# Keys of the fourth head between the second and third score tile of each attention block

## Chip, cores and metric

The kernel runs on one core of a Trainium2 chip. The metric is the device time of one execution in microseconds (us), the median of several. The engines are TensorE (PE; its weight loads are shown apart as PEld), VectorE (DVE), ScalarE (ACT), GpSimd (POOL) and SyncE (SP), which here issues the loads of the weights.

## The reference

Four graph layers run one after another over 625 nodes with 512 features and 20,000 edges; each takes a normalised copy of `x` and adds its result to it. The change lies in the third, which has four blocks with attention of four heads of 128 features. One block, cut:

```python
y = cond_layer_norm(x, cond, ...)                    # scale and bias made from a condition
q = (y @ wq + bq).reshape(N, H, Dh) * Dh ** (-0.5)
k = (y @ wk + bk).reshape(N, H, Dh)
v = (y @ wv + bv).reshape(N, H, Dh)
scores = einsum('ehd,ehd->eh', q[src], k[dst])       # one score per edge and head
attn = softmax of the scores over the edges of one src
out = segment_sum(attn[:, :, None] * v[dst], src)
x = x + out.reshape(N, D) @ wo + bo
y = cond_layer_norm(x, cond, ...)
x = x + relu(y @ m_w1 + m_b1) @ m_w2 + m_b2
```

## The kernel before

The edge sums are done densely: an earlier stage builds a 625 x 625 matrix of edge counts, and attention is that of all nodes to all nodes with a mask made of the logarithm of the counts. Nodes come in five tiles of up to 128 (`NT = 5`), features in four (`KT = 4`); a head is one feature tile. Every fp32 product is made of three passes: each operand is kept as a rounded high part and a low part (the rest), and high x high, high x low and low x high are summed. So every operand that is made on the chip costs a copy on ACT (high) and a subtraction on DVE or POOL (low).

The third layer is `pe_l2`, `act_l2`, `dve_l2` and `pool_l2`: one program for each engine, a loop over four blocks (`it`), written out in full, each with its own fixed order. Semaphores that only count up tie them: `big_full` (PE has filled a PSUM buffer), `big_read` (DVE has read it), `split_done` (the low part of a weight tile is there), `shi_up` (its high part is), `qkhi_up`, `exp_up`, `rden_up`, `pn_up` and others. Three large PSUM buffers are used in turn, in the order of one list, `BLOCK_BIG`; use number u waits until use u-3 has been read (`free_big`).

In a block, PE makes the values, then eight projections q0 to q3 and k0 to k3 (one head each, 24 matmuls), then goes through the list `ATT`, which `attention_order(True)` builds. It has, for 20 tiles (head, node tile), a score tile S (6 matmuls), three steps behind it the transposes T of the same tile's probabilities (5 matmuls), and for each head two products with the values, PVa and PVb. It starts S0, S1, S2, S3, T0, S4, T1, S5, ... ACT follows `ATT_ACT`, where T comes ahead of S in a step: S0, S1, S2, T0, S3, T1, ...

What one tile passes through: PE scores; DVE adds the mask, writes the tile to `pbuf` and keeps its minimum (L2073); ACT takes exp with the sum of the rows (L1473); DVE inverts the sum (L2078), placed behind the next tile's L2073; POOL scales the tile (L1268, it counts `pn_up`); PE transposes it (L1649, waits for `pn_up`); ACT copies the high part (L1478) and DVE takes the low part (L2082).

A projection passes through ACT (L1465, high part with the bias) and DVE (L2062, low part). The weights come by DMA into four staging buffers, ACT copies the high part into a ring of six slots (`high`, L1514), POOL makes the low part (`rest`, L1327). In ACT's program each of the eight projections is followed by one such copy: WK2, WK3, WO0 to WO3, W1_0 and, behind k3, W1_1 (tile 1 of `m_w1`). In POOL's program these low parts, W1_1 the last of them, stand ahead of the loop over the 20 scalings:

```python
                rests(WO + NT - 2, 0, KT + 4 - NT)
                for k in range(HEADS * NT):
                    wait_apart(g, rden_up, it * HEADS * NT + k + 1)
```

(WO3, W1_0 and W1_1 are made in the first line.) SP loads a weight tile as soon as the low part of the tile four places ahead of it has been made (`stage`).

Of the kernel before, what the change touches and what calls it, by code (L numbers as in the profile page):

```python
# [13 lines left out]
ALU = mybir.AluOpType  # L14
# [27 lines left out]
HEADS = 4  # L42
# [31 lines left out]
def attention_order(scores_first):  # L74
# [4 lines left out]
    for k in range(HEADS * NT + LAG):  # L79
# [3 lines left out]
        for what, behind in (("PVa", PVA_AT), ("PVb", PVB_AT)):  # L83
            if kk >= behind and (kk - behind) % NT == 0:
# [2 lines left out]
    return steps + [("PVb", HEADS - 1)]  # L87


ATT = attention_order(True)  # L90
ATT_ACT = attention_order(False)


BLOCK_BIG = (FIRST_NORM + [f"q{h}" for h in range(HEADS)] + [f"k{h}" for h in range(HEADS)]
             + [f"{a}{b}" for a, b in ATT] + norm_order(1) + [f"m{o}" for o in range(KT)])
L3_BIG = [f"l3_{t}" for t in range(NT)] + ["asr"]

# [57 lines left out]
def wide(ap640):  # L155

    return ap640[:, 0:NW].rearrange("p (h n) -> p h n", h=2)
# [6 lines left out]
def build(nc, a, out):  # L164
    ctx = ExitStack()
    with ctx:
# [147 lines left out]
        def bwide(u):  # L314
            return big[buf(u)][:, :, 0:HW]
# [1113 lines left out]
        def act_l2(act, high):  # L1429
            def turned(ln, t, b):  # L1430
                act_turned(act, ln, t, b)

            for it in range(BLOCKS):
                nb, nr = it * len(BLOCK_BIG), it * len(BLOCK_ROW)

                def highs(q, first, last):
                    for i in range(first, last):
                        high(S_BLK + q + i, ringpart(RING_BLK + q + i)[0], it)

                def value(t):  # L1440
                    act.wait_ge(row_read, ROWBLK[f"v{t}"] + nr + 1)
                    act.activation(vrow[:, 0, t, :], vbuf[:, t % 2, :], ACT.Copy).then_inc(vhi_up, 1)

                if it:
                    act.wait_ge(row_full, ROWB + nr)
                    highs(WV, 2, KT)
                    turned(0, 1, it)
                    act.wait_ge(row_read, ROWB + nr)
                    act_bias(act, it)
                    highs(WQ, 0, 1)  # L1450
                    turned(0, 2, it)
                    highs(WQ, 1, 2)
                for t in range(NT):
                    value(t)
                    if t + 3 < NT + (not it):
                        turned(0, t + 3 - (not it), it)
                    if not it and t < 2:
                        highs(WQ, t, t + 1)
                highs(WQ, 2, KT)
                highs(WK, 0, 2)  # L1460
                for i, to in enumerate((qT, kT)):
                    for h in range(HEADS):
                        u = BIGBLK["qk"[i] + str(h)]
                        act.wait_ge(big_full, u + nb + 1)
                        act.activation(wide(to[:, 0, h, :]), bwide(u), ACT.Identity,  # L1465
                                       bias=bqk[:, i, bass.ds(it * KT + h, 1)]).then_inc(qkhi_up, 1)
                        n = i * HEADS + h + 2
                        highs((WK, WO, W1)[n // KT], n % KT, n % KT + 1)

                for what, k in ATT_ACT:  # L1470
                    if what == "S":
                        act.wait_ge(big_read, BIGBLK[f"S{k}"] + nb + 1)
                        act.activation(pbuf[:, k % 4, 0:NW], pbuf[:, k % 4, 0:NW], ACT.Exp, bias=nsmax[:, k:k + 1],  # L1473
                                       scale=-1.0, accum_out=den[:, k:k + 1]).then_inc(exp_up, 1)
                    elif what == "T":
                        u = BIGBLK[f"T{k}"]
                        act.wait_ge(big_full, u + nb + 1)
                        act.activation(pT[:, 0, :, (k % NT) * P:(k % NT + 1) * P], bflat(u).rearrange("p (k n) -> p k n", k=NT),  # L1478
                                       ACT.Copy).then_inc(phi_up, 1)
                    else:  # L1480
                        u, at = BIGBLK[f"{what}{k}"], PV_COLS[what]
                        act.wait_ge(big_full, u + nb + 1)
                        act.activation(qT[:, 0, k, at], big[buf(u)][:, 0, 0:at.stop - at.start], ACT.Copy).then_inc(ohi_up, 1)
                for t in range(NT):
                    turned(1, t, it)
                    if t == 2:
                        act.wait_ge(row_full, ROWBLK["wo4"] + nr + 1)
                    if t >= 2:
                        highs((W1, W1, W2)[t - 2], (2, 3, 0)[t - 2], (3, 4, 1)[t - 2])
                highs(W2, 1, 2)  # L1490
                if it == BLOCKS - 1:
                    act.wait_ge(big_read, BIGBLK[f"S{HEADS * NT - 1}"] + nb + 1)
                    for t in range(NT):
                        act.activation(mask[:, t, :], mask[:, t, :], ACT.Identity, bias=flag[:, 3, t:t + 1], scale=DH ** -0.5).then_inc(m3_up, 1)


                for o in range(KT):
                    act.wait_ge(big_read, BIGBLK[f"m{o}"] + nb + 1)
                    act.activation(kT[:, 0, o, 0:NW], rbuf[:, o % 2, 0:NW], ACT.Copy).then_inc(hhi_up, 1)
                    if o < 2:  # L1500
                        highs(W2, 2 + o, 3 + o)
                    for i in ((), (), (0,), (1, 2, 3))[o] if it < BLOCKS - 1 else ():
                        high(S_BLK + PERBLK + i, condw[:, i, :], it)
                if it < BLOCKS - 1:
                    for i in range(2):
                        high(S_BLK + S_PERBLK + i, ringpart(RING_BLK + i)[0], it)
                    turned(0, 0, it + 1)
# [174 lines left out]
        def pe_l2(pe, turn_norm):  # L1682
# [6 lines left out]
            for it in range(BLOCKS):  # L1689
# [20 lines left out]
                turn_y(0, 4, it)  # L1710
                for t in (3, 4):
                    values(t)
                for i in range(2):
                    for h in range(HEADS):
                        u = BIGBLK["qk"[i] + str(h)]
                        free_big(pe, u, nb)
                        q = (WQ, WK)[i] + h
                        pe.wait_ge(split_done, S_BLK + q + 1 + ns)
                        wide_mm(pe, u, sum([parts(wcol(RING_BLK + q, k), both(yT, k)) for k in range(KT)], [])).then_inc(big_full, 1)
                def row_terms(name, t, left, w, pieces):  # L1720

                    pe.wait_ge(split_done, S_BLK + w + pieces[-1] + 1 + ns)
# [21 lines left out]
                for what, k in ATT:  # L1744

                    if (what, k) == ("PVa", HEADS - 1):
                        row_begin("wo", 0, qT, WO)
                    elif (what, k) == ("PVb", HEADS - 1):
                        out_end(0)
                        row_begin("wo", 1, qT, WO)  # L1750
                    u = BIGBLK[f"{what}{k}"]
                    free_big(pe, u, nb)
                    if what == "S":
                        h, t = k // NT, k % NT
                        pe.wait_ge(big_read, BIGBLK[f"k{h}"] + nb + 1)
                        wide_mm(pe, u, parts(nodes_of(qT, h, t), both(kT, h))).then_inc(big_full, 1)
                    elif what == "T":
                        pe.wait_ge(pn_up, it * HEADS * NT + k + 1)
                        turn(pe, u, pbuf[:, k % 4, :], NT).then_inc(big_full, 1)
                    else:  # L1760
                        at = PV_COLS[what]
                        last = k * NT + at.stop // P - 1
                        pe.wait_ge(big_read, BIGBLK[f"T{last}"] + nb + 1)
                        pe.wait_ge(vlo_up, (it + 1) * NT)
                        row_mm(pe, big[buf(u)][:, 0, 0:at.stop - at.start],
                               sum([parts([vrow[0:KEYS[st], s, st, k * DH:(k + 1) * DH] for s in range(2)],
                                          [pT[0:KEYS[st], s, st, at] for s in range(2)]) for st in range(NT)], [])).then_inc(big_full, 1)
# [234 lines left out]
        def dve_l2(dve, tile_sums, tile_moments, tile_stats, entry_stats, f32, relu_rest, l3_norm):  # L2002
            dve.wait_ge(mask_up, NT)
            norm_tile, centred, scaled, turned_rest = dve_first(dve, f32)
            for it in range(BLOCKS):
# [49 lines left out]
                    turned_rest(0, t, it)  # L2055
                    values(t - 1)
                values(4)
                for i, to in enumerate((qT, kT)):
                    for h in range(HEADS):
                        u = BIGBLK["qk"[i] + str(h)]  # L2060
                        dve.wait_ge(qkhi_up, it * 2 * HEADS + i * HEADS + h + 1)
                        dve.scalar_tensor_tensor(wide(to[:, 1, h, :]), bwide(u), bqk[:, i, bass.ds(it * KT + h, 1)],  # L2062
                                                 wide(f32(to[:, 0, h, :])), ALU.add, ALU.subtract).then_inc(big_read, 1)
                heads = it * HEADS * NT
                for what, k in ATT + [("last", 0)]:
                    if what == "S":
                        u = BIGBLK[f"S{k}"]
                        t = k % NT
# [456 lines left out]
```

## Time and profile before

| | us |
|---|---|
| runs | 952.76, 954.74, 957.96 |
| median | 954.74 |
| the profiled execution | 953.18 |
| its span | 951.3 |
| PE busy | 850.3 (89%) |
| DVE busy | 660.6 (69%) |
| POOL busy | 515.8 (54%) |
| ACT busy | 457.3 (48%) |

The mean granted clock of TensorE was 0.964 of full speed. The four blocks lie between about 190 and 825 us of the span. The view of waits tells who released an engine that stood idle; the timeline gives each engine's instructions in order of time, with the idle time ahead of them; the view of windows gives busy time and clock of a stretch.

### The profile page before, as it was taken

The page shows a single profiled execution, that of the slowest core. Times are in us where ns is not written, and L with a number is a line of the kernel's source. Part 1 is how long each engine was busy: PE and PEld are TensorE (multiplying, and loading weights), DVE is VectorE, ACT ScalarE, POOL GpSimd, SP SyncE. Part 2 cuts the span into 40 slices and gives each one's busy share as a digit, 9 for nine tenths or more (in the row PEclk, how much of TensorE's full clock was granted, in tenths as well). Part 3 has the DMA queues.
Part 4 walks back from the last instruction along what each step waited for, and adds up shares of the span by engine and source line. Part 5 has one row for each costly group of instructions (what it writes and reads, how often), then busy time and mean ns, then how long its engine had stood idle before and what let it go on. Part 6 is the DMA issues. An engine that isn't in the chain of part 4 may idle for free.

```text
span 951.3 us, 18275 instructions
## 1 busy us (share of the span) xinstructions
PE 850.3 (89%) x6760; PEld 744.5 (78%) x6760; DVE 660.6 (69%) x1305; ACT 457.3 (48%) x764; POOL 515.8 (54%) x601
## 2 busy tenths in 40 slices
PE   3899869989999899999988999989999998888886
PEld 2788757878998787989786989878798978765456
DVE  8999888782466685266676346577427667679896
ACT  5777563233565233466233456423437615245664
POOL 7677624257632466843176753256674319447771
PEclk9999978999999999999999999999999999978899
DMA  5000001142200024300016220002330002100111
GB/s 131 32 0 0 23 23 23 47 100 78 79 1 1 23 70 111 111 23 2 1 36 169 75 67 1 2 23 80 100 114 21 1 1 78 34 1 29 43 57 55
DMA packets 49362, 44.34 MB, mean 47 GB/s; under 512 B 6014, under 2 KB 37154, under 8 KB 49300
## 3 DMA queue, kind: packets, MB, share of 16 engines
q1 hardware_dynamic: 47492, 40.21, 14.7%
q10 hardware_dynamic: 1808, 3.31, 1.8%
q8 instruction: 38, 0.62, 0.3%
q14 instruction: 24, 0.20, 0.1%
HBM read 42.04 MB, written 1.33 MB: 46 GB/s over the span
## 4 chain that ended last, share of the span: by engine, by line
PE 61%; DVE 21%; issue 6%; ACT 5%; POOL 3%; DVEq 2%; DMA 2%; ACTq 0%; SPq 0%; POOLq 0%
PE psum L1631 24%; PE psum L1625 16%; PE psum L1725 11%; PE psum L1649 5%; DVE arena L2082 2%; ACT arena L1478 2%; DMA bias<-in_L_gnn_m_b 2%; PE psum L849 1%; DVE arena L927 1%; DVE stats L2210 1%; PE psum L1673 1%; DVE hot_dst L964 1%; DVEq L2314 1%; DVE hot_dst L2309 1%; DVE xn L2223 1%
## 5 line engine op out<-in xcount | busy, mean ns | idle before, releaser
L1268 POOL TENSOR_SCALAR acc<-acc,rden,flag 128x628 f32<-128x628 f32 x80 | 69.8, 873 | 111.0 <-DVE rden L2078 110.5
L1725 PE MATMUL psum<-ringw,arena 128*128 128x512 f32 (+1 forms) x480 | 119.0, 397 | 3.7 <-DVE arena L2090 2.5
L1631 PE MATMUL psum<-arena 128*128 128x384 f32 (+5 forms) x675 | 115.7, 324 | 0.0
L1631 PE MATMUL psum<-ringw,arena 128*128 128x512 f32 (+1 forms) x418 | 99.7, 391 | 17.0 <-POOL ringw L1327 5.2
L1625 PEld LDWEIGHTS psum<-arena,ringw 128*128 128x128 f32 x768 | 113.0, 190 | 0.4
L1625 PE MATMUL psum<-arena,ringw 128*128 128x314 f32 x768 | 113.3, 309 | 0.0
L1631 PEld LDWEIGHTS psum<-arena 128*128 128x128 f32 (+1 forms) x675 | 105.0, 189 | 6.7 <-DVE arena L2082 1.1
L1725 PEld LDWEIGHTS psum<-ringw,arena 128*128 128x128 f32 (+1 forms) x480 | 86.9, 186 | 24.8 <-DVE arena L2090 3.5
L1631 PEld LDWEIGHTS psum<-ringw,arena 128*128 128x128 f32 x418 | 75.3, 203 | 34.1 <-issue 15.4
L1649 PE MATMUL psum<-ident,acc 128*128 128x128 f32 (+1 forms) x560 | 81.0, 275 | 19.1 <-DVE acc L1991 15.3
L1625 PE MATMUL psum<-arena 128*128 128x314 f32 (+1 forms) x480 | 88.2, 322 | 6.3 <-DVE arena L2082 5.6
L2062 DVE SCALAR_TENSOR_TENSOR arena<-psum,cols,arena 128x628 fp32r<-128x628 f32 x32 | 27.9, 872 | 88.0 <-ACT arena L1465 88.0
L1649 PEld LDWEIGHTS psum<-ident,acc 128*128 128x128 f32 (+1 forms) x560 | 65.9, 140 | 28.6 <-DVE acc L1991 18.7
L1327 POOL TENSOR_TENSOR ringw<-raw,ringw 128x512 fp32r<-128x512 f32 x56 | 72.2, 1297 | 28.7 <-ACT ringw L1514 28.7
L1320 POOL TENSOR_SCALAR veps<-mv 128x1 f32<-128x1 f32 x60 | 14.4, 240 | 131.9 <-DVE mv L2214 130.4
L1625 PEld LDWEIGHTS psum<-arena 128*128 128x128 f32 (+1 forms) x480 | 70.3, 187 | 15.0 <-DVE arena L2082 13.0
L2082 DVE TENSOR_TENSOR arena<-psum,arena 128x640 fp32r<-128x640 f32 x80 | 65.0, 817 | 15.8 <-ACT arena L1478 15.8
L1378 POOL TENSOR_TENSOR hot_dst<-hot_dst,w_part 128x160 bf16<-128x160 bf16 x120 | 58.2, 512 | 27.0 <-DVE hot_dst L2309 27.0
L1327 POOL TENSOR_TENSOR ringw<-xn,ringw 128x512 fp32r<-128x512 f32 x49 | 64.9, 1338 | 11.1 <-ACT ringw L1514 10.9
L1473 ACT ACTIVATE acc<-acc,nsmax 128x628 f32<-128x628 f32 x80 | 65.2, 815 | 9.2 <-DVE nsmax L2073 8.2
L2073 DVE CUSTOM_DVE_ANT_0 acc<-psum,mask 128x628 f32<-128x628 f32 x80 | 63.8, 801 | 0.0
L1631 PE MATMUL psum<-arena,ringw 128*128 128x314 f32 x384 | 62.1, 327 | 0.0
(283 smaller groups left out, 1834.2 us busy)
## 6 DMA issues: line engine op xcount, KB each, us to landing
raw<-in_L_gnn_m_w SPq DMA_DIRECT2D x16, 256.0 KB
xn<-in_L_gnn_m_w SPq DMA_DIRECT2D x16, 256.0 KB
raw<-in_L_gnn_wv SPq DMA_DIRECT2D x8, 256.0 KB
xn<-in_L_gnn_wv SPq DMA_DIRECT2D x8, 256.0 KB
raw<-in_L_gnn_wq SPq DMA_DIRECT2D x8, 256.0 KB
xn<-in_L_gnn_wq SPq DMA_DIRECT2D x8, 256.0 KB
raw<-in_L_gnn_wk SPq DMA_DIRECT2D x8, 256.0 KB
xn<-in_L_gnn_wk SPq DMA_DIRECT2D x8, 256.0 KB
```

What stands on the lines that cost most here:

```text
L1268: g.tensor_scalar(pbuf[:, k % 4, 0:NW], pbuf[:, k % 4, 0:NW], rden[:, k:k + 1], flag[:, 1, k % NT:k % NT + 1], ALU.mult, ALU.mult).then_in ...
L1327: g.tensor_tensor(to[1], staged[slot(n)], to[0].bitcast(F32), ALU.subtract).then_inc(split_done, 1)
L1378: ins = g.tensor_tensor(hot_dst[:, b, :, (i + 1) * WIN:(i + 2) * WIN], hot, w_part[:, i, :, bass.ds(gr, 1)].broadcast_to([P, CH, WIN]), AL ...
L1473: act.activation(pbuf[:, k % 4, 0:NW], pbuf[:, k % 4, 0:NW], ACT.Exp, bias=nsmax[:, k:k + 1], scale=-1.0, accum_out=den[:, k:k + 1]).then_ ...
L1478: act.activation(pT[:, 0, :, (k % NT) * P:(k % NT + 1) * P], bflat(u).rearrange("p (k n) -> p k n", k=NT), ACT.Copy).then_inc(phi_up, 1)
L1625: ins = pe.matmul(big[buf(u)][0:l.shape[1], h, 0:HW], l, r[:, h * HW:(h + 1) * HW], start=(i == 0), stop=(i == len(terms) - 1))
L1631: ins = pe.matmul(to, l, r, start=(i == 0), stop=(i == len(terms) - 1))
L1649: ins = pe.transpose(bflat(u)[0:KEYS[k], k * P:(k + 1) * P], src[:, k * P:k * P + KEYS[k]], ident[:, :])
L1725: ins = pe.matmul(brow(ROWBLK[f"{name}{t}"])[0:KEYS[t], :], l, r, start=(pieces[0] + i == 0), stop=(pieces[-1] == KT - 1 and i == len(term ...
L2062: dve.scalar_tensor_tensor(wide(to[:, 1, h, :]), bwide(u), bqk[:, i, bass.ds(it * KT + h, 1)], wide(f32(to[:, 0, h, :])), ALU.add, ALU.sub ...
L2073: dve.tensor_tensor_reduce(wide(pbuf[:, k % 4, :]), bwide(u), wide(mask[:, t, :]), -DH ** -0.5, 3e38, ALU.add, ALU.min, nsmax[:, k:k + 1]) ...
L2082: dve.tensor_tensor(pT[:, 1, :, t * P:(t + 1) * P], bflat(u).rearrange("p (k n) -> p k n", k=NT), f32(pT[:, 0, :, t * P:(t + 1) * P]), ALU ...
```

## The change

k3, the keys of the last head, leaves the row of projections and becomes a step of the attention lists, between S1 and S2. In `BLOCK_BIG` it moves the same way. The body of a projection becomes a function on PE, ACT and DVE, called in the loop over `QK` (now seven) and in the loop over `ATT` or `ATT_ACT`. On ACT that body includes the weight copy that follows a projection. `pool_l2` and SP's program are not touched.

```diff
+
 ATT = attention_order(True)
+ATT.insert(2, ("k", HEADS - 1))
 ATT_ACT = attention_order(False)
-
-
-BLOCK_BIG = (FIRST_NORM + [f"q{h}" for h in range(HEADS)] + [f"k{h}" for h in range(HEADS)]
+ATT_ACT.insert(2, ("k", HEADS - 1))
+QK = [("q", h) for h in range(HEADS)] + [("k", h) for h in range(HEADS - 1)]
+
+
+BLOCK_BIG = (FIRST_NORM + [f"q{h}" for h in range(HEADS)] + [f"k{h}" for h in range(HEADS - 1)]
              + [f"{a}{b}" for a, b in ATT] + norm_order(1) + [f"m{o}" for o in range(KT)])
...
-                for i, to in enumerate((qT, kT)):
-                    for h in range(HEADS):
-                        u = BIGBLK["qk"[i] + str(h)]
-                        act.wait_ge(big_full, u + nb + 1)
-                        act.activation(wide(to[:, 0, h, :]), bwide(u), ACT.Identity,
-                                       bias=bqk[:, i, bass.ds(it * KT + h, 1)]).then_inc(qkhi_up, 1)
-                        n = i * HEADS + h + 2
-                        highs((WK, WO, W1)[n // KT], n % KT, n % KT + 1)
+                def projected(what, h):
+                    i, to = {"q": (0, qT), "k": (1, kT)}[what]
+                    u = BIGBLK[f"{what}{h}"]
+                    act.wait_ge(big_full, u + nb + 1)
+                    act.activation(wide(to[:, 0, h, :]), bwide(u), ACT.Identity,
+                                   bias=bqk[:, i, bass.ds(it * KT + h, 1)]).then_inc(qkhi_up, 1)
+                    n = i * HEADS + h + 2
+                    highs((WK, WO, W1)[n // KT], n % KT, n % KT + 1)
+
+                for what, h in QK:
+                    projected(what, h)
 
                 for what, k in ATT_ACT:
-                    if what == "S":
+                    if what == "k":
+                        projected(what, k)
+                    elif what == "S":
...
-                for i in range(2):
-                    for h in range(HEADS):
-                        u = BIGBLK["qk"[i] + str(h)]
-                        free_big(pe, u, nb)
-                        q = (WQ, WK)[i] + h
-                        pe.wait_ge(split_done, S_BLK + q + 1 + ns)
-                        wide_mm(pe, u, sum([parts(wcol(RING_BLK + q, k), both(yT, k)) for k in range(KT)], [])).then_inc(big_full, 1)
+                def projected(what, h):
+                    u = BIGBLK[f"{what}{h}"]
+                    free_big(pe, u, nb)
+                    q = {"q": WQ, "k": WK}[what] + h
+                    pe.wait_ge(split_done, S_BLK + q + 1 + ns)
+                    wide_mm(pe, u, sum([parts(wcol(RING_BLK + q, k), both(yT, k)) for k in range(KT)], [])).then_inc(big_full, 1)
+
+                for what, h in QK:
+                    projected(what, h)
...
+                    if what == "k":
+                        projected(what, k)
+                        continue
                     u = BIGBLK[f"{what}{k}"]
                     free_big(pe, u, nb)
...
+                for what, h in QK:
+                    projected(what, h)
                 heads = it * HEADS * NT
                 for what, k in ATT + [("last", 0)]:
+                    if what == "k":
+                        projected(what, k)
                     if what == "S":
```

(The last piece is DVE's; its `projected` holds the wait for `qkhi_up` and the instruction of L2062, unchanged.)

## Rows read from the trace of the kernel before

**Rows 1.** The page: its head and its part 1 (busy time, share, instructions).

```profile
span 951.3 us, 18275 instructions
...
PE 850.3 (89%) x6760; PEld 744.5 (78%) x6760; DVE 660.6 (69%) x1305; ACT 457.3 (48%) x764; POOL 515.8 (54%) x601
```

**Rows 2.** The page, part 4: the chain that ended last, by engine.

```profile
PE 61%; DVE 21%; issue 6%; ACT 5%; POOL 3%; DVEq 2%; DMA 2%; ACTq 0%; SPq 0%; POOLq 0%
```

**Rows 3.** Timeline of PE, block 1: start, us, engine, line, operation, [idle before, releaser].

```profile
377.39 28.32 PE L1625 MATMUL psum<-arena,ringw 128*128 128x314 f32 x192
405.55 3.93 PE L1625 MATMUL psum<-arena 128*128 128x314 f32 x24
410.44 0.74 PE L1649 MATMUL psum<-ident,acc 128*128 128x128 f32 x5 [0.95 <-POOL acc L1268]
```

**Rows 4.** Waits of PE, whole span: total us, times, longest us.

```profile
PE psum L1649 <- POOL acc L1268: 3.9, 4, 1.1
```

**Rows 5.** Timeline of PE, start of attention in blocks 0 and 3.

```profile
252.47 3.97 PE L1625 MATMUL psum<-arena 128*128 128x314 f32 x24
257.52 0.74 PE L1649 MATMUL psum<-ident,acc 128*128 128x128 f32 x5 [1.08 <-POOL acc L1268]
...
717.68 0.74 PE L1649 MATMUL psum<-ident,acc 128*128 128x128 f32 x5 [0.93 <-POOL acc L1268]
```

**Rows 6.** Timeline of ACT: one row of block 0, three of block 1.

```profile
253.99 1.28 ACT L1473 ACT_TABLE_LOAD   x1
...
405.75 0.79 ACT L1465 ACTIVATE arena<-psum,cols 128x628 fp32r<-128x628 f32 x1 [2.22 <-PE psum L1625]
406.43 0.62 ACT L1514 ACTIVATE ringw<-raw 128x512 fp32r<-128x512 f32 x1
408.20 0.82 ACT L1473 ACTIVATE acc<-acc,nsmax 128x628 f32<-128x628 f32 x1 [1.15 <-DVE nsmax L2073]
```

**Rows 7.** Timeline of DVE, block 1.

```profile
406.57 0.87 DVE L2062 SCALAR_TENSOR_TENSOR arena<-psum,cols,arena 128x628 fp32r<-128x628 f32 x1 [2.65 <-ACT arena L1465]
407.36 0.80 DVE L2073 CUSTOM_DVE_ANT_0 acc<-psum,mask 128x628 f32<-128x628 f32 x1
...
409.15 0.16 DVE L2078 RECIPROCAL rden<-den 128x1 f32<-128x1 f32 x1 [0.25 <-ACT acc L1473]
```

**Rows 8.** Timeline of POOL, block 1 (the last row holds three scalings).

```profile
407.13 1.29 POOL L1327 TENSOR_TENSOR ringw<-raw,ringw 128x512 fp32r<-128x512 f32 x1 [2.23 <-ACT ringw L1514]
409.42 2.73 POOL L1268 TENSOR_SCALAR acc<-acc,rden,flag 128x628 f32<-128x628 f32 x3 [1.00 <-DVE rden L2078]
```

**Rows 9.** Timeline of SP's queue, block 1: first and last issue and the next.

```profile
404.93 3.86 SPq L1159 DMA_DIRECT2D raw<-in_L_gnn_m_w  x2
479.68 1.57 SPq L1159 DMA_DIRECT2D xn<-in_L_gnn_m_w  x2
```

**Rows 10.** Chain of work, block 1, behind the first transposes: start, us, what.

```profile
411.21 0.72 ACT arena L1478
411.95 0.84 DVE arena L2082
412.83 1.14 PE psum L1625 x6
```

**Rows 11.** Windows: length, busy us by engine, PEclk, DMA share, GB/s.

```profile
405.55:410.44 4.89, 3.91 (x27) 3.43 (x25) 3.62 (x10) 3.40 (x7) 2.31 (x3) 1.00 0.29 101
429.79:442.42 12.63, 12.16 (x87) 11.53 (x86) 8.92 (x23) 8.47 (x18) 4.38 (x6) 1.00 0.01 2
480.00:484.00 4.00, 4.00 (x20) 4.00 (x19) 0.89 (x2) 1.64 (x3) 4.00 (x4) 0.57 0.46 131
512.00:516.00 4.00, 2.24 (x9) 1.44 (x9) 3.96 (x7) 1.57 (x3) 3.82 (x5) 1.00 0.74 173
875.00:878.00 3.00, 1.70 (x8) 0.86 (x6) 2.96 (x7) 1.98 (x3) 3.00 (x3) 1.00 0.05 2
878.00:883.00 5.00, 4.67 (x15) 2.58 (x15) 4.53 (x13) 2.47 (x4) 3.17 (x3) 0.66 0.00 1
```

**Rows 12.** Timeline of PE, block 1: the product with `m_w1`.

```profile
480.13 15.69 PE L1631 MATMUL psum<-arena,ringw 128*128 128x314 f32 x96
```

More of the change, by code:

```diff
@@ L2057, in dve_l2, with projected @@
                 values(4)
[L2058 to L2063, printed above, removed]
+                def projected(what, h):
+                    i, to = {"q": (0, qT), "k": (1, kT)}[what]
+                    u = BIGBLK[f"{what}{h}"]
+                    dve.wait_ge(qkhi_up, it * 2 * HEADS + i * HEADS + h + 1)
+                    dve.scalar_tensor_tensor(wide(to[:, 1, h, :]), bwide(u), bqk[:, i, bass.ds(it * KT + h, 1)],
+                                             wide(f32(to[:, 0, h, :])), ALU.add, ALU.subtract).then_inc(big_read, 1)
+                for what, h in QK:
+                    projected(what, h)
                 heads = it * HEADS * NT
                 for what, k in ATT + [("last", 0)]:
+                    if what == "k":
+                        projected(what, k)
                     if what == "S":
```

## The prediction

> **What bounds the kernel now.** I read the page's head and its chain first. TensorE (PE) is busy for 89% of a 951.3 us span, and 61% of the chain that ended last lies on it [rows 1, 2]. So the first question for any edit is what it does to PE's idle time. Next I read PE's timeline around the start of attention in block 1 [rows 3]. The eight projections of q and k run from 377.39 to 405.55 without a gap, 28.16 us, so 3.52 us each. The first score tiles S0 to S3 take 3.93 us, 0.98 each. Then PE stands still for 0.95 us until the first transpose T0 starts at 410.44, released by GpSimd (POOL), which has to scale the first probability tile. The view of waits says the same of all four blocks: four such stalls, 3.9 us in all, 1.1 the longest [rows 4]; blocks 0 and 3 show 1.08 and 0.93 [rows 5]. This one stall per block is all that the change can win here: once T0 runs, PE is busy for 12.16 of 12.63 us in a later stretch of the same loop [rows 11].
>
> **Why T0 is late.** I take the other engines' rows of block 1 and count each from the start of S0 (405.55), which is also the end of the last projection. ScalarE (ACT) turns out k3's high part at +0.20, then makes the high part of the weight tile W1_1 at +0.88 and takes exp of S0 at +2.65 [rows 6]. VectorE (DVE) makes k3's low part at +1.02, reduces S0 at +1.81 and inverts its sum at +3.60 [rows 7]. POOL makes the low part of W1_1 at +1.58 (1.29 us long) and scales tile 0 at +3.87 [rows 8]; T0 follows the start of that scaling by 1.02, at +4.89. The projection k3 and its two copies thus stand ahead of S0 on DVE and ACT, and PE has only S1 to S3 to cover the chain from S0 to T0.
>
> **The change, part by part.** I count from the end of k2 (E2), where S0 now starts. Before, T0 starts at E2 + 3.52 + 4.89 = 8.41; in block 0, where S0 starts at 252.47 and T0 at 257.52 [rows 5], at 3.52 + 5.05 = 8.57.
> - *PE order.* S0 and S1 end at 1.97, k3 at 1.97 + 3.52 = 5.49, S2 and S3 at 7.45. k3 needs k2's PSUM buffer read: DVE's copy ends 1.02 + 0.87 = 1.89 after k2, so in time. Nothing is added; the same instructions run in another order, at zero cost in PE's work. As cover for the chain from S0 it is ideal.
> - *DVE and ACT.* S0's chain is as before (exp +2.65, inverse +3.60), now counted from E2, while PE works on k3. k3's high part falls at 5.49 + 0.20 = 5.69, its low part at 6.51 to 7.38, S2's reduction directly behind it, done near 8.2, S3's near 9.0. On ACT, exp of S1 is done by about 4.5, so it delays nothing, and in block 0 the table load of 1.28 us [rows 6] lies there too, hidden by k3. There is only one such load at the exponentials, so mixing Identity and exp costs nothing further.
> - *The copy of W1_1 moves with k3.* In ACT's program each projection is followed by one weight copy; k3's is W1_1. It now comes after exp of S1 and after k3's own copy. POOL's program is unchanged: it has the low part of W1_1 ahead of the scaling of tile 0. So POOL waits for ACT's copy with tile 0's scaling queued behind that wait, and PE's T0 waits for the scaling. This is the wait that takes the place of the one removed. POOL can start W1_1 at 5.49 + 1.58 = 7.07, ends it at 8.36 and starts scaling then; T0 starts 1.02 later, at 9.38.
> - *Sum.* 9.38 against 8.41 is +0.97 us in blocks 1 to 3, against 8.57 it is +0.81 in block 0: 3 x 0.97 + 0.81 = +3.7 us. PE's idle time ahead of T0 becomes 9.38 - 7.45 = 1.93 us where it was 0.95. The bounds of POOL's turn-round are -0.05 (back-to-back instructions overlap a little) to +0.1 (the gap of 0.10 us between the inverse and the scaling in [rows 7, 8], if it comes on top), so the sum lies between +3.5 and +4.1.
> - *After T0.* The next late step hangs on T0 itself: ACT copies it at +0.77, DVE takes the rest at +1.51 and S5 starts at +2.39 [rows 10]; so the loop runs the same distance behind T0 as before. Nothing is won back there: S2 and S3 are reduced before T0 in both orders.
> - *SP's queue.* The load of the tile W2_1 waits for W1_1's buffer and goes out about 2 us later against the end of the projections. It is in the pair issued from 404.93 on [rows 9], and no other load of the weights is issued in the trace until 479.68, some 70 us later, so that is covered. Were it not, it would cost those 2 us at W2 at most.
> - *Clock.* The longer stall could drop PE's granted clock. At the present stall of 0.95 it stays at 1.00 [rows 11], and so it does over 512 to 516, where PE is idle for 1.76 of 4.00 us. It falls, to 0.57 over 480 to 484, behind a passage in which PE waits for DVE; and to 0.66 over 878 to 883, where the 3 us before held 1.30 idle and work on a part of the array. So the cost is between nothing and a fall to the lower level (1.2 of 2.4 GHz) in each block. That is worth 15.69 - 96 x 28.32/192 = 1.53 us [rows 3, 12]. I take nothing, since the row of 512 to 516 is nearest in idle time, and keep 4 x 1.53 = 6.1 for the range.
>
> The page "TensorE: Matmul & The Clock Gate" of the Trainium skill, section "Architectural detail: the array is 16x 32x32, not 1x 128x128", says that the queues of ACT and GpSimd are strictly first in, first out; by it tile 0's scaling can't slip past W1_1, by a rule of freer order the saving of the second rival would stand. [...]
>
> **Rivals.**
> - *The clock falls in the stall ahead of T0* (slower by over 0.5%). Its place is the 1.93 us idle before T0 in each block; its price 1.53 us where it happens, and it decides once it happens in one or more blocks: +3.7 + 1.53 = +5.2 with one, +9.8 with all four, near 964. For it: the fall near 878 behind only 1.30 us idle [rows 11]. Against it: 512 to 516, and that full-array work stands directly on both sides of the stall.
> - *The cover works and POOL doesn't hold it back* (faster). T0 would start as soon as PE has done S3, at 7.45: -0.96 in three blocks, -1.12 in block 0, -4.0 us, near 950. For it: S0's chain is done by then, as its scaling could start at 3.87. Against it: POOL's place for W1_1, which would have to be reached before ACT's copy. I see no way to that.
> - *The change moves nothing measurable* (-1 to +1 us): POOL's delay is taken up again in the loop, as POOL is busy for only 4.38 of 12.63 us there. Against it: the loop is tied to T0 by ACT and DVE, not to POOL.
>
> **How the numbers follow.** The profiled execution took 953.18 us, 1.9 more than its span; with +3.7 it is 956.9. The median of the runs shown is 954.74, with +3.7 it is 958.4. I take the middle, 957.6. Chances: forecast 0.72, clock 0.15, nothing 0.08, cover works 0.05. About 0.5% (4.8 us) is what a measurement of this kernel can tell from no change, and my sum lies below that. Slower by over that: the clock rival's 0.15, and 0.05 for the upper end of the sum. Faster by over it: 0.02, as even the full saving of 4.0 stays under the bound. Within: 0.78. The range reaches from 952.5 (no effect, with the spread of the runs from 952.76 to 957.96) to 964.0 (the clock falling in all four blocks, 957.6 + 6.1).
>
> **What would show it.** In the changed kernel: POOL's low part of W1_1 starts some 1.6 us after k3's end and tile 0's scaling directly behind it, without a wait; PE's idle time before T0 is near 1.9 us and is still put down to POOL's scaling; S0's exp lies under k3 on PE; the tile loop from T0 on has the same spacing; the clock over it is 1.00. Wrong would be a T0 directly behind S3, a clock under 1.00 after T0, or a stall of PE ahead of k3.

## The result: 965.6 us against 953.8, outside the range

The changed kernel took 965.64 us (median of 4 runs, 962.75 to 967.94), the kernel before 953.75 beside it: ratio 1.0112, interval 1.0088 to 1.0136. A later measurement gave 1.0119 (1.0102 to 1.0136). So it is slower by some 11 us where 3.7 were forecast, and lies above the range's upper end of 964.0. The profiled execution took 967.94 us, its span 966.1.

The page of the changed kernel, its head, part 1, and the row of granted clock of part 2 (40 slices of the span, in tenths):

```profile
span 966.1 us, 18275 instructions
...
PE 859.2 (89%) x6760; PEld 753.4 (78%) x6760; DVE 659.9 (68%) x1305; ACT 457.0 (47%) x764; POOL 513.9 (53%) x601
...
PEclk9999989999999899999999999989999998988899
```

The instructions are the same 18275. DVE, ACT and POOL are busy for as long as before, to 2 us [rows 1]; PE is busy for 9 us longer with the same 6760 matmuls. That is the first sign of a lower clock; the other 6 us of the longer span are idle time. PE's timeline at the start of attention in block 1, the rows that answer to [rows 3]:

```profile
406.95 1.92 PE L1634 MATMUL psum<-arena 128*128 128x314 f32 x12
408.90 3.78 PE L1634 MATMUL psum<-arena,ringw 128*128 128x314 f32 x24
412.52 1.92 PE L1634 MATMUL psum<-arena 128*128 128x314 f32 x12
416.37 1.14 PE L1658 MATMUL psum<-ident,acc 128*128 128x128 f32 x5 [1.94 <-POOL acc L1272]
417.16 1.92 PE L1634 MATMUL psum<-arena 128*116 128x314 f32 x6
```

S0 and S1, k3, S2 and S3, then 1.94 us idle, then T0. T0 and S4, behind it, last 1.14 and 1.92 us; the same two steps took 0.74 and 1.11 to 1.12 us in the kernel before and in block 0 of this one. The view of waits of PE, the answer to [rows 4]:

```profile
PE psum L1658 <- POOL acc L1272: 7.8, 4, 2.0
```

And POOL's timeline, the answer to [rows 8]:

```profile
414.10 1.27 POOL L1331 TENSOR_TENSOR ringw<-raw,ringw 128x512 fp32r<-128x512 f32 x1 [4.28 <-ACT ringw L1523]
415.36 2.57 POOL L1272 TENSOR_SCALAR acc<-acc,rden,flag 128x628 f32<-128x628 f32 x3
```

POOL stands for 4.28 us in front of W1_1, and the scalings follow it without a wait. DVE had inverted tile 0's sum long before (the answer to the last of [rows 7]):

```profile
410.55 0.16 DVE L2098 RECIPROCAL rden<-den 128x1 f32<-128x1 f32 x1 [0.25 <-ACT acc L1482]
```

That is 3.60 us after the start of S0, as forecast, and 4.8 us before the scaling starts.

**Where the time is.** I laid the traces side by side at fixed points of each block: the first projection (P), T0, the start of the last group of ident transposes of attention (TL), the product with `m_w1` (M), the product with `m_w2` behind it, and the next block's P. Three traces of each kernel stand behind the table (the two profiled ones and those of later runs); each entry is the sum of a stretch over the four blocks (three for the last but one), mean of three traces, in us.

| stretch | before | after | more |
|---|---|---|---|
| start to P of block 0 | 224.7 | 224.9 | 0.2 |
| P to T0 | 132.3 | 136.1 | 3.8 |
| T0 to TL | 184.9 | 188.3 | 3.4 |
| TL to M | 94.5 | 94.7 | 0.3 |
| M | 61.8 | 64.2 | 2.5 |
| behind M to the next P | 107.4 | 108.7 | 1.3 |
| behind the last M to the end | 148.2 | 148.2 | 0.0 |

The sum is 11.5. The two profiled executions alone differ by 14.8, of which 1.75 arise before the first block, where the kernels are the same.

P to T0 is the wait that was forecast. The rest lies in stretches in which TensorE's granted clock is lower for longer: from T0 to TL it is at the lower level for 10.2 us in each trace of the changed kernel, and never in the kernel before. Windows of the changed kernel (length, busy us by engine, PEclk, DMA share, GB/s): T0 of block 0, T0 of block 1, and the start of M in block 0, where the kernel before has 0.57 over the four us of its fall:

```profile
259.00:263.00 4.00, 2.64 (x19) 2.42 (x20) 2.21 (x5) 2.94 (x6) 2.68 (x4) 1.00 0.23 66
416.00:420.00 4.00, 3.63 (x17) 3.62 (x18) 1.76 (x5) 1.58 (x4) 1.93 (x3) 0.57 0.27 70
326.00:334.00 8.00, 5.19 (x23) 5.01 (x24) 4.46 (x8) 2.75 (x5) 6.63 (x7) 0.61 0.20 66
```

Each fall in the blocks goes to the lower level (1.2 of 2.4 GHz) and lasts 3.4 us, or 6.8. The changed kernel falls behind T0 in blocks 1, 2 and 3 in all three traces, never in block 0; the kernel before never does.

### The profile page after: what moved, and what is told of

It is laid out like the page before. It is cut to its first block, busy times and chain, and to the rows that moved or that the text cites. A ratio compares the mean times of both kernels' runs of the same rounds, so it can differ in the third digit from the quotient of the medians.

```text
span 966.1 us, 18275 instructions
## 1 busy us (share of the span) xinstructions
PE 859.2 (89%) x6760; PEld 753.4 (78%) x6760; DVE 659.9 (68%) x1305; ACT 457.0 (47%) x764; POOL 513.9 (53%) x601
## 4 chain that ended last, share of the span: by engine, by line
PE 59%; DVE 19%; POOL 6%; issue 6%; ACT 4%; DVEq 3%; DMA 1%; SPq 1%; ACTq 0%; POOLq 0%
PE psum L1640 23%; PE psum L1634 17%; PE psum L1737 9%; PE psum L1658 5%; POOL ringw L1331 3%; DVE arena L2102 2%; ACT arena L1487 2%; DVE arena L931 1%; PE psum L853 1%; PE psum L1682 1%; DVE stats L2230 1%; DVEq L2334 1%; DVE hot_dst L2329 1%; DVE hot_dst L968 1%; DVE z L2327 1%
## 5 line engine op out<-in xcount | busy, mean ns | idle before, releaser
L1737 PE MATMUL psum<-ringw,arena 128*128 128x512 f32 (+1 forms) x480 | 119.1, 397 | 4.2 <-DVE arena L2110 2.5
L1640 PE MATMUL psum<-ringw,arena 128*128 128x512 f32 (+1 forms) x418 | 105.2, 407 | 17.0 <-POOL ringw L1331 6.5
L1634 PE MATMUL psum<-arena,ringw 128*128 128x314 f32 x768 | 114.2, 310 | 0.1
L1640 PEld LDWEIGHTS psum<-arena 128*128 128x128 f32 (+1 forms) x675 | 104.9, 189 | 7.7 <-DVE arena L2102 1.1
L1640 PEld LDWEIGHTS psum<-ringw,arena 128*128 128x128 f32 x418 | 79.9, 214 | 34.7 <-issue 15.3
L1658 PE MATMUL psum<-ident,acc 128*128 128x128 f32 (+1 forms) x560 | 83.9, 282 | 22.5 <-DVE acc L2006 14.7
L1634 PE MATMUL psum<-arena 128*128 128x314 f32 (+1 forms) x480 | 90.6, 328 | 5.5 <-DVE arena L2102 5.3
L1658 PEld LDWEIGHTS psum<-ident,acc 128*128 128x128 f32 (+1 forms) x560 | 68.6, 145 | 31.6 <-DVE acc L2006 17.1
L1634 PEld LDWEIGHTS psum<-arena 128*128 128x128 f32 (+1 forms) x480 | 73.3, 194 | 12.6 <-DVE arena L2102 11.6
L1426 ACT ACTIVATE arena<-psum 128x512 fp32r<-128x512 f32 x40 | 23.8, 594 | 85.4 <-PE psum L1658 85.3
L1640 PE MATMUL psum<-arena,ringw 128*128 128x314 f32 x384 | 64.1, 334 | 0.0
```

What stands on the lines that cost most here:

```text
L1426: act.activation(yT[:, 0, :, t * P:(t + 1) * P], bflat(u)[:, 0:D].rearrange("p (k n) -> p k n", k=KT), ACT.Copy).then_inc(yhi_up, 1)
L1634: ins = pe.matmul(big[buf(u)][0:l.shape[1], h, 0:HW], l, r[:, h * HW:(h + 1) * HW], start=(i == 0), stop=(i == len(terms) - 1))
L1640: ins = pe.matmul(to, l, r, start=(i == 0), stop=(i == len(terms) - 1))
L1658: ins = pe.transpose(bflat(u)[0:KEYS[k], k * P:(k + 1) * P], src[:, k * P:k * P + KEYS[k]], ident[:, :])
L1737: ins = pe.matmul(brow(ROWBLK[f"{name}{t}"])[0:KEYS[t], :], l, r, start=(pieces[0] + i == 0), stop=(pieces[-1] == KT - 1 and i == len(term ...
```

## The experiments

My theory after the result: (1) POOL's order sets T0, (2) the clock falls because PE then stands idle, and (3) neither needs k3 to be where it is. The rivals: DVE or ACT hold T0, as k3 is in their queues too; the fall comes from the kind of work; the later falls are chance.

### Both kernels again

> The kernel before, once more, for its clock. Theory A (the further falls of the clock belong to the change): the trace shows the lower level for about 68 us in all as the first one, none behind T0 and none at the start of a block's values. Theory B (they depend on how the falls happen to lie in an execution): other places, and a total that differs by 10 us or more between two executions of one kernel.

It took 955.63 us. No fall behind T0; a fall at the end of block 0 that the first trace doesn't have; 56 us at the lower level in all, against 68 in the first.

> The changed kernel once more. Both theories: 1.94 us idle ahead of T0 in each block, as that is set by the order of POOL. Theory A: the clock falls behind T0 in three or four blocks again and the lower level lasts about 88 us in all. Theory B: it falls there in one or two blocks or none, and the total lies elsewhere between 68 and 95 us.

965.87 us, idle time ahead of T0 as before, falls behind T0 in blocks 1 to 3, 92 us at the lower level. So neither theory in its pure form: the falls behind T0 belong to the change and come back in the same blocks; the total over the span differs by 12 us between the two executions of the kernel before.

> The kernel before, a third trace, to part chance from the change in the later stages. If the longer falls of the clock at the product with m_w1 belong to the change, the four stretches of that product take 61 to 62 us in all here, as in the two earlier traces (61.9, 60.7), against 63.6 to 64.6 of the changed kernel. If they are chance, this trace may show 63 or more.

957.81 us. The four M take 62.6 us, between the two groups, with one long fall of 6.8 us in block 1. So long falls at M are possible without the change.

> The changed kernel in five rounds beside the kernel before, for the size of the loss. From the two traces of each: longer waits ahead of T0 3.7 us, falls of the clock behind T0 3.3 us, longer falls at the product with m_w1 about 2.7, later parts of the blocks about 1.4: 11 us, ratio 1.0115. If the last two are chance of single executions, the ratio is near 1.0075.

Ratio 1.0119 (1.0102 to 1.0136), 968.06 against 956.42: the larger figure holds. Its four M take 64.6 us (64.5 and 63.6 in the two earlier traces), T0 to TL 188.3 as in those.

### POOL's order

```diff
-                rests(WO + NT - 2, 0, KT + 4 - NT)
+                rests(WO + NT - 2, 0, KT + 3 - NT)
                 for k in range(HEADS * NT):
+                    if k == 1:
+                        rests(W1, 1, 2)
```

> The changed kernel with POOL's low part of W1_1 put behind the scaling of tile 0 instead of ahead of it. Theory 1 (POOL's queue holds T0 back): T0 follows S3 at once, the stall ahead of T0 is under 0.2 us and no fall of the clock starts there. T1 then waits: the inverse of tile 1 stands behind S2's reduction on DVE, about 8.3 us after the end of k2, so T1 starts near 9.4 and some 0.4 us per block remain of the 0.96 against before. Time 2 us under before (near 952), some 14 under the changed kernel. Rival (T0 is held by DVE or ACT, whose queues also got k3 ahead of S2): the stall stays at 1.5 us or more and the time stays near 965.

Ratio 0.9977 (0.9963 to 0.9992) with 955.81 against 957.22: faster than the kernel before. Its PE in block 1, from S2 and S3 on, and its POOL:

```profile
409.92 1.92 PE L1636 MATMUL psum<-arena 128*128 128x314 f32 x12
411.87 0.77 PE L1660 MATMUL psum<-ident,acc 128*128 128x128 f32 x5
```

```profile
408.23 0.86 POOL L1274 TENSOR_SCALAR acc<-acc,rden,flag 128x628 f32<-128x628 f32 x1 [1.00 <-DVE rden L2100]
411.51 1.27 POOL L1333 TENSOR_TENSOR ringw<-raw,ringw 128x512 fp32r<-128x512 f32 x1 [2.41 <-ACT ringw L1525]
412.77 1.87 POOL L1274 TENSOR_SCALAR acc<-acc,rden,flag 128x628 f32<-128x628 f32 x2
```

POOL scales tile 0 while PE works on k3, and T0 follows S3 at once. P to T0 is 32.14 us against 33.04, T0 to TL 46.9 against 46.2, as tile 1's scaling now waits for W1_1. No clock falls behind T0. DVE and ACT, whose order was left, didn't hold T0: that rival is out. Over the four blocks P to TL is 1.0 us shorter than in the kernel before; the ratio says 2.2, and the rest of the lead isn't placed.

> The kernel before with POOL's low part of W1_1 behind the scaling of tile 0, k3 in its old place. If the lead of the kernel with POOL's order changed came from that order itself, this is faster by some 2 us too. Mine: it does nothing, as POOL stands idle for 1.0 us there between W1_1 and the scaling: stall ahead of T0 0.95 us, ratio 1.000 within 0.002.

Ratio 1.0009 (0.9988 to 1.0030). The order of POOL alone gains nothing; it needs k3 in its new place. T0 to TL is longer by 0.26 us a block here. The four M take 63.4 us in this trace, although nothing that idles PE was added.

### The wait moves with k3

k3 is put one place later, behind S2 (`insert(3, ...)` in both lists), POOL as in the changed kernel.

> k3 behind S2 as in the better kernel, but POOL's order as it was, W1_1 ahead of tile 0's scaling. Theory (the wait follows k3 through the copy of W1_1): POOL starts W1_1 1.58 us after the end of k3 (6.47 us after k2), ends it at 9.34 and T0 starts at 10.36, with 2.9 us idle ahead of it: 1.95 us later than in the kernel before in each block, 7.7 us in all, falls of the clock behind T0 in three or four blocks (3.3 to 4.4 us) and more later, 968 to 974. Rival (some other chain holds T0): T0 no later than in the changed kernel.

966.19 against 956.54 us, ratio 1.0110 (1.0066 to 1.0153). T0 of block 1:

```profile
416.41 1.30 PE L1658 MATMUL psum<-ident,acc 128*128 128x128 f32 x5 [2.81 <-POOL acc L1272]
```

The cause is confirmed: k3 one place later makes the stall longer by 0.9 us, one score tile. P to T0 grows by 1.8 us over the kernel before where I had 1.95. The clock falls at T0 in all four blocks, in blocks 1 to 3 within the stall itself, and twice for 6.8 us: T0 to TL costs 6.5 us more than before, where 3.3 to 4.4 were forecast. The time is still lower than forecast (it rests on two runs), as the later stages had few falls: M takes 62.1 us in all, and the stretch behind the last M 145.5 against 148.2.

### Idle time without k3

The kernel before, with two instructions of no use on POOL:

```diff
                 rests(WO + NT - 2, 0, KT + 4 - NT)
+                for i, c in enumerate([512, 256]):
+                    g.tensor_tensor(rbuf[:, i, 0:c], z[:, 0, 0:c], z[:, 1, 0:c], ALU.subtract)
```

> The kernel before, its order unchanged, with two instructions of no use (512 and 256 columns, 1.3 and about 0.65 us) on POOL behind the low part of W1_1 and ahead of the scaling of tile 0. They end about 1 us after the scaling could have started, so PE stands still for about 1.9 us ahead of T0, as in the changed kernel. Theory 1 (it is the idle time alone that counts, not where k3 is made): 3.8 us for the waits, and the clock falls behind T0 in some blocks, some 3 us more: 960 to 965 against 954 to 957. Rival (the fall needs k3 between the score tiles): no fall behind T0, only the 3.8 us.

> The same with 512 and 128 columns: about 0.6 us later, so 1.5 us idle ahead of T0. Theory 1 with a fall that needs nearly 2 us of idle time: +2.4 us and no fall behind T0. If the clock falls here too, the bound lies between 0.95 and 1.5 us.

> The kernel before with two idle instructions of 512 columns on POOL ahead of the scaling of tile 0: about 2.5 us idle ahead of T0, +6 us for the waits. If a longer stall means a surer fall, the clock falls behind T0 in block 0 too (four falls, 4.4 us). If block 0 is spared again, it is not the length of the stall that spares it.

T0 of block 1 in the kernels late by half, by one and by two:

```profile
414.21 0.74 PE L1651 MATMUL psum<-ident,acc 128*128 128x128 f32 x5 [1.58 <-POOL acc L1270]
```

```profile
415.23 1.18 PE L1651 MATMUL psum<-ident,acc 128*128 128x128 f32 x5 [1.88 <-POOL acc L1270]
```

```profile
416.79 1.29 PE L1651 MATMUL psum<-ident,acc 128*128 128x128 f32 x5 [2.40 <-POOL acc L1270]
```

| kernel | idle ahead of T0, block 1 | falls behind T0 | ratio to before |
|---|---|---|---|
| before | 0.95 | none | 1 |
| late by half | 1.58 | none | 1.0058 (1.0038 to 1.0077) |
| late by one | 1.88 | blocks 1 to 3 | 1.0083 (1.0063 to 1.0104) |
| changed kernel | 1.94 | blocks 1 to 3 | 1.0119 (1.0102 to 1.0136) |
| late by two | 2.40 | all four | 1.0119 (1.0070 to 1.0168) |
| k3 behind S2, POOL old | 2.81 | all four | 1.0110 (1.0066 to 1.0153) |

So idle time alone makes the clock fall, with k3 in its old place, in the same blocks as in the changed kernel. Ahead of T0 the step lies between 1.6 and 1.9 us in blocks 1 to 3, and block 0 follows with a longer stall; each kernel that was added has one trace, and the last two ratios rest on two runs each. The length isn't all that decides: block 0 holds its clock behind 1.86 us (late by one) and 1.94 to 1.97 (changed kernel), and at other places of the program shorter pieces are followed by a fall (below). In its trace the kernel late by one copies the changed kernel stretch by stretch (P to T0 33.98 us, T0 to TL 47.3 in blocks 1 to 3). That execution is the slowest of its four, though, and the median is 965.50 us where the changed kernel has 968.06 beside the same kernel before. So it is shown that the falls come from the idle time, and not that the whole loss does. Late by half was forecast at +2.4 us; it has no fall behind T0 and still lost 5.5. Its trace has two falls of 6.8 us at M, 63.6 us in all.

### The stall filled

```diff
                     elif what == "T":
+                        if k == 0:
+                            row_mm(pe, big[buf(u)][:, 0, 0:HW], [(yT[:, 0, 0, 0:P], yT[:, 0, 0, 0:HW])] * 12)
                         pe.wait_ge(pn_up, it * HEADS * NT + k + 1)
```

> The changed kernel with 12 matmuls of 314 columns of no use (about 1.8 us at full clock) put ahead of T0, into the buffer that T0 then overwrites. PE is busy where it stood idle, nothing else moves. If the clock's fall behind T0 comes from the idle time: no fall there, and the stretch from T0 to the last transposes is as long as in the kernel before (46.3 us) in all blocks; the time falls by 3.3 us and by what of the later falls hangs on it, to 957 to 962. If the fall hangs on something else (the kind of work ahead of it), it stays and the time is 965 or a little more.

Ratio 1.0061 (1.0043 to 1.0079), 962.76 against 957.22 us, where the changed kernel has 1.0119; the forecast was 957 to 962. Block 1:

```profile
413.21 2.01 PE L1640 MATMUL psum<-arena 128*128 128x314 f32 x12
415.06 0.76 PE L1658 MATMUL psum<-ident,acc 128*128 128x128 f32 x5
```

T0 comes as late as in the changed kernel (P to T0 33.97 us), but from T0 to TL all four blocks take 46.2: work of no use that keeps PE from idling wins back half the loss. It still loses 5.8 us where the waits are 3.6. The other 2.2 aren't placed: its trace is of one of the two fastest of ten executions (958.65 us). In it the stretches from TL to the next P are longer than before, by 2.4 us in all, and the stretch behind the last M is shorter by 2.9.

### The better version

k3 behind S2, and POOL's low part of W1_1 behind the scaling of tile 1 (`if k == 2`).

> The changed kernel with k3 one place later, behind S2 instead of S1, on all engines, and POOL's low part of W1_1 behind the scaling of tile 1. T0 directly behind S3 (7.45 us after the end of k2, before 8.41), the inverse of tile 1 no longer behind k3 on DVE, so T1 near 9.3. S4 waits for k3's buffer to be read, till 8.4. S5 near 10.3 instead of 10.8: 0.5 us per block, 2 us in all under the kernel before, ratio 0.998. Rival (the loop takes every lead back, as DVE and ACT bound the first tiles): ratio 1.000.

Ratio 0.9968 (0.9955 to 0.9982), 954.10 against 956.42 us: faster than both kernels. PE in block 1:

```profile
410.34 1.04 PE L1636 MATMUL psum<-arena 128*128 128x314 f32 x6
411.22 0.71 PE L1660 MATMUL psum<-ident,acc 128*128 128x128 f32 x5
412.29 1.13 PE L1636 MATMUL psum<-arena 128*116 128x314 f32 x6 [0.36 <-DVE arena L2079]
```

T0 follows S3; S4 waits 0.36 us for k3's buffer, as worked out. P to T0 is 31.97 us against 33.04 and T0 to TL 46.4 against 46.2, which is 0.87 us a block and 3.5 in all; the ratio says 3.1. The lead is kept by the loop, so the rival (DVE and ACT take it back) is out.

## Why the prediction was wrong

- *PE's order, DVE and ACT*: right. S0's chain took 3.60 us to the inverse, k3 started without a wait, and DVE and ACT delayed nothing.
- *The copy of W1_1 moves with k3 and holds tile 0's scaling*: right, in mechanism and size. POOL started W1_1 7.15 us after E2 (406.95) where 7.07 was worked out, T0 came 9.42 after it (9.38), idle 1.94 (1.93). Measured 3.8 us, forecast 3.7.
- *After T0*: right on the order of work (PE's steps have the same distances in block 0), wrong on time, by the next point.
- *Clock*: this is the step that failed. I took nothing, by the row of 512 to 516, in which PE is idle for 1.76 of 4.00 us at full clock, in two pieces of 0.48 and 1.28 us. That row was one place in one execution. The third trace of the kernel before has the same two pieces at the same place, and there the clock falls: the same 12 matmuls take 4.58 us (timeline of PE, first trace and third):

```profile
514.66 3.01 PE L1631 MATMUL psum<-ringw,arena 128*128 128x512 f32 x12 [1.28 <-POOL ringw L1327]
```

```profile
518.50 4.58 PE L1631 MATMUL psum<-ringw,arena 128*128 128x512 f32 x12 [1.30 <-POOL ringw L1327]
```

  In the changed kernel the pair (0.47 to 0.49 and 1.28 to 1.39 us) is followed by a fall in all nine cases of three traces. So the row couldn't carry a cost of nothing. The trace I had also holds rows ahead of the first block that I had not used (timeline of PE; window behind the second row):

```profile
204.75 2.98 PE L1631 MATMUL psum<-ringw,arena 128*128 128x512 f32 x12 [2.64 <-POOL ringw L1327]
...
219.91 4.58 PE L1631 MATMUL psum<-ringw,arena 128*128 128x512 f32 x12 [1.88 <-DVE arena L1997]
```

```profile
220.00:224.00 4.00, 4.00 (x11) 3.11 (x12) 0.36 (x1) 0.63 (x1) 1.27 (x1) 0.59 0.02 4
```

  The same 12 matmuls take 2.98 us behind an idle piece of 2.64 and 4.58 behind one of 1.88: the clock fell there behind one piece as long as the stall I had forecast, and didn't behind a longer one. With the fall behind 1.30 in the row of 878, I would now give it at least an even chance, not 0.15. What the runs showed in place of nothing: three falls behind T0, 3.4 us in all. The price I had given a fall was somewhat high: a fall behind T0 costs 1.1 us (T0 to TL 47.3 against 46.2) and not 1.53. PE's own idle time in the loop shrinks by 0.1 to 0.3 us under the lower clock; the rest of the difference I didn't take apart.
- *What I had no term for*: the falls at M are longer (64.2 against 61.8 us) and those ahead of the next block's projections come in three blocks of three (in one of three in the second and in the third trace of before, in none in the first). Together 3.8 us. The change idles PE nowhere near them; the fall at M exists in both kernels (in all blocks but one of the second trace of before), behind the same two waits. What goes with a long one can be read: where the fall begins behind the start of M or up to 1.45 us ahead of it, it is over after 3.4 us; where it begins 1.47 us or more ahead it lasts 6.8, in all fourteen traces. What they don't show is why the changed kernel should meet the longer case more often. Kernels with longer blocks and no fall behind T0 (late by half, stall filled) lost 2.9 and 2.2 us beyond their waits, and the kernel with POOL's order alone, which lost nothing, had 63.4 us at M. The fastest kernel of all (k3 behind S2, POOL's order changed) has 63.4 us at M too, and a fall ahead of the projections in three blocks of three, with none behind T0: these falls aren't tied to the stall at T0. This part stays open: it is measured in the ratio, but not tied to a cause.
- *The range*: its upper end came from four falls at T0, and 964.0 would have held the 3.8 and 3.4 us had the open part not come on top.
- *Rivals*: "nothing measurable" and "the cover works" were wrong for the changed kernel. The second became true as soon as POOL's one line was moved, and gave 0.2 to 0.9 us a block instead of the 1.0 reckoned, since tile 1's scaling (or k3's buffer) is late next.

## What to carry to other kernels

When a step is moved on some engines, follow every instruction that rides with it, and ask for each engine that was not touched what in its fixed order waits for one of them: here one weight copy on ACT held up POOL, and POOL the whole loop. Price a new stall of TensorE twice, as idle time and as a possible fall of its clock behind it. Look at every place of the trace with idle time of such a size and at how long the same matmuls take behind it, in more than one execution if there is one: a single place where the clock held shows little, as the same pieces were followed by a fall in another execution. And where the cost is a wait in another engine's queue, look for the one line to reorder there: the same change with that line moved was faster than the kernel it started from.

## What the runs showed of the hardware

- Ahead of T0, between dense fp32 matmuls, an idle piece of 1.58 us left TensorE's granted clock at 1.00 in four blocks of one trace. One of 1.85 to 1.97 us was followed by the lower level in blocks 1 to 3 of four traces and in block 0 of none, one of 2.40 us in all four blocks of its trace.
- The length of a piece doesn't settle it. The pair of 0.48 and 1.28 to 1.39 us ahead of a block's values was followed by a fall in nine of nine cases in the changed kernel and in one of six in the kernel before (its other three have a longer second piece of 1.60 to 1.79 us, with one fall). The piece of 2.64 us ahead of the first block was followed at once by a fall in one trace of the kernel before, 1.3 us later in another, and in the third it wasn't. What else decides stays open. Each fall in the blocks lasted 3.4 us or 6.8.
- A lower clock costs less than its length: 3.4 us at half clock cost 1.1 us in the attention loop, where PE had small waits of its own.
- Filling the stall with matmuls of no use was worth about 0.6% of the kernel's time (1.0061 against 1.0119).
- The time at the lower level over the whole span differed between executions of the same kernel from 56 to 72 us (before, three traces) and from 89 to 99 us (changed, three traces).
